# Two-layer decoder, last stage: masks and exponential sums of the attention scores move from TensorE to VectorE and ScalarE

## Chip, cores and metric

One Trainium2 chip, one of its cores. The metric is the device time of one launch in microseconds; less is better. A measurement is the median of several runs.

## The reference

Six residual sublayers over `x` (8 batches of 256 tokens, 512 wide, fp32), each followed by a layer norm: differential attention, a long convolution, a mixture of experts, causal attention with 16 heads, cross attention to a context, and a causal attention whose 16 heads share one key and value per token, chosen by a gate. The change is in the fourth and the sixth:

```python
scores = jnp.einsum('bhqd,bhkd->bhqk', q, k) * HD ** (-0.5)
scores = jnp.where(causal, jnp.float32(-1000000000.0), scores)
a = jax.nn.softmax(scores, axis=-1)
ctx = jnp.einsum('bhqk,bhkd->bhqd', a, v)
...
att = jnp.einsum('bhqd,bkd->bhqk', q, k_shared) * (1.0 / math.sqrt(hd))
att = jnp.where(causal[None, None, :, :], att, -jnp.inf)
att = jax.nn.softmax(att, axis=-1)
y = jnp.einsum('bhqk,bkd->bhqd', att, v_shared)
```

## The kernel before

The kernel runs five stages one after the other. The last one (`tail_stage`) does sublayers four to six from about 1180 us of the span to its end. It treats a batch of 256 tokens as a unit. P is the causal attention of the fourth sublayer, C the cross attention, H the gate and the shared keys and values of the sixth, A the attention over them. They are staggered: round r works on batch r of P, r - 1 of C, r - 2 of H and r - 3 of A. The loop `for r in range(2, B)` holds the rounds 2 to 7; rounds 0 and 1 and the end (A5, A6, A7 among it) are written out by hand.

Each engine has its own program, with the same rounds in an order written by hand, and waits on semaphores. TensorE writes to PSUM: four banks called `ring` that are claimed in turn for projections, transposes and weighted sums (a claim waits until the bank's last content was drained), and one group of four banks, `scores`, claimed by `quads`.

A unit of P or A has 16 heads in four blocks of four (`c`), each block with these steps:

- `score` (L1865 on): 16 small bf16 products by `add_masks` (L123) write the causal mask into `scores`, products of 256 (L1883) and 128 columns (L1886) add query times key. Queries lie on the partitions. The four heads of a block stand on four strips of 32 rows and run side by side; each fp32 product is two records in the trace.
- `maxima` (VectorE, L2603 and L2604): the negated row maxima into `negtop`, and the bank is released.
- After four blocks `split_top` (VectorE) writes the maxima as two bf16 parts, `shift` (TensorE, L1893) turns them, `take_shift` (ScalarE) copies them to `shiftT`.
- `scoreT` (L1905, L1909, L1912) computes the scores again with the keys on the partitions, with the shift added by a product with `pick16`. `exps` (ScalarE, L2394) takes their exponentials into `expT`. `causal` (GpSimd) zeroes the masked entries (L2310) and adds the two key halves of the later queries (L2315).
- `weigh` multiplies by the values (L1932), and by 32 columns of ones (L1935): these are the sums of the exponentials. `mix` (VectorE) takes their reciprocals (L2615) and multiplies (L2616) into `mixedT`.

Other steps named below: `cols` and `rows` are the projections (L191, L198), `turn` a transpose of a batch (L1848), `shared_out` the transposes of A's result, `cross_turn` those of C's probabilities, `turned` a wait for ScalarE's two copies of a turn. `norm` (L2583) applies a layer norm whose root comes from GpSimd (`root`, L2302); `gate_choice` (from L2631), `pick` and `gate_value` build the shared key and value on VectorE and drain H's banks. At the head of the stage GpSimd fetches rows, fills `pick16` by eight dependent selects (L2327), and only then does the first root.

## Time and profile before

| | |
|---|---|
| median of 3 runs | 2128.2 us (2126.52 to 2128.36) |
| span of the profiled execution | 2127.3 us |
| TensorE busy | 97% |
| VectorE busy | 53% |
| ScalarE busy | 24% |
| GpSimd busy | 27% |

The span is from the first to the last instruction of the profiled execution. TensorE's busy time is a union of records whose ends are modelled, so steps of TensorE are better measured from the start of one to the start of the next. A number in brackets behind an instruction is the engine's idle time before it, and what ended that.

### The profile page before, as it was taken

The page shows a single profiled execution, that of the slowest core. Times are in us where ns is not written, and L with a number is a line of the kernel's source. Part 1 is how long each engine was busy: PE and PEld are TensorE (multiplying, and loading weights), DVE is VectorE, ACT ScalarE, POOL GpSimd, SP SyncE. Part 2 cuts the span into 40 slices and gives each one's busy share as a digit, 9 for nine tenths or more (in the row PEclk, how much of TensorE's full clock was granted, in tenths as well). Part 3 has the DMA queues.
Part 4 walks back from the last instruction along what each step waited for, and adds up shares of the span by engine and source line. Part 5 has one row for each costly group of instructions (what it writes and reads, how often), then busy time and mean ns, then how long its engine had stood idle before and what let it go on. Part 6 is the DMA issues. An engine that isn't in the chain of part 4 may idle for free. (4 is left out here: it accounts for less than half of the span.)

```text
span 2127.3 us, 32323 instructions
## 1 busy us (share of the span) xinstructions
PE 2057.7 (97%) x13439; PEld 1194.6 (56%) x13439; DVE 1128.4 (53%) x1731; ACT 518.8 (24%) x791; POOL 580.5 (27%) x548
## 2 busy tenths in 40 slices
PE   7899999999999999999999999999999999999996
PEld 5444444334444557556566655766666666666664
DVE  2567777567777744122222334364646464736567
ACT  2445555440000121101011122122222222222211
POOL 2222222128999600111110312022222222121122
PEclk9999999999999999999999999999999999999998
DMA  5101111205111147321211602100010101000000
GB/s 161 48 1 55 55 56 45 87 38 210 40 43 44 35 156 277 126 65 65 65 65 55 222 3 99 50 31 21 17 44 1 60 1 41 1 31 12 1 11 21
DMA packets 66237, 130.81 MB, mean 61 GB/s; under 512 B 6480, under 2 KB 19920, under 8 KB 66096
## 3 DMA queue, kind: packets, MB, share of 16 engines
q1 hardware_dynamic: 45968, 77.49, 11.1%
q10 hardware_dynamic: 14448, 32.64, 4.3%
q0 software_dynamic: 5680, 18.62, 3.0%
q8 instruction: 111, 1.82, 0.4%
q14 instruction: 30, 0.25, 0.0%
HBM read 97.40 MB, written 41.81 MB: 65 GB/s over the span
## 5 line engine op out<-in xcount | busy, mean ns | idle before, releaser
L1033 PE MATMUL conv_conv<-kv,toep 128*128 128x512 f32 x576 | 247.6, 592 | 0.3 <-POOL kv L1067 0.3
L2615 DVE RECIPROCAL tail_inv<-tail_ring 128x256 f32<-128x256 f32 x63 | 110.7, 1757 | 188.8 <-PE tail_ring L1935 188.3
L1623 PE MATMUL moe_gu_ps<-gu,xT_tile 128*128 x608 | 192.4, 459 | 0.0
L1033 PEld LDWEIGHTS conv_conv<-kv,toep 128*128 128x128 f32 x576 | 109.4, 190 | 139.0 <-issue 129.6
L1067 POOL TENSOR_TENSOR kv<-vT,cT 128x512 f32<-128x512 f32 x128 | 147.0, 1172 | 15.8 <-PE conv_conv L1033 12.0
L2302 POOL TENSOR_TENSOR tail_rstd_x<-tail_rstd_x,const_minus_half 128x2 f32<-128x2 f32 x31 | 21.8, 702 | 469.6 <-DVE tail_rstd_x L2577 469.6
L1623 PEld LDWEIGHTS moe_gu_ps<-gu,xT_tile 128*128 128x128 f32 x608 | 112.3, 190 | 66.5 <-issue 17.8
L2310 POOL TENSOR_SCALAR_AFFINE_SELECT tail_expT<-tail_expT 128x1024 f32<-128x1024 f32 x64 | 71.5, 1119 | 242.1 <-ACT tail_expT L2394 242.0
L2603 DVE TENSOR_REDUCE tail_negtop<-tail_scores 128x4 f32<-128x1024 f32 x64 | 78.2, 1221 | 95.6 <-PE tail_scores L1886 95.4
L594 POOL TENSOR_SCALAR_AFFINE_SELECT front_expT<-front_expT 128x2048 f32<-128x2048 f32 x32 | 64.3, 2008 | 199.1 <-ACT front_expT L649 199.1
L1604 POOL DMA_INDIRECT xg<-x_after,tokens x37 | 35.0, 947 | 282.3 <-PE moe_xT_ps L1618 255.2
L1705 DVE TENSOR_TENSOR moe_hid<-moe_gu_ps,moe_silu 128x352 f32<-128x352 f32 x39 | 20.5, 525 | 170.7 <-PE moe_gu_ps L1623 170.7
L649 ACT ACTIVATE front_expT<-front_scores 128x2048 f32<-128x2048 f32 x48 | 90.1, 1878 | 78.3 <-PE front_scores L367 78.3
L1651 PE MATMUL moe_y_ps<-down,moe_hT 128*128 (+1 forms) x234 | 107.1, 593 | 0.7 <-ACT moe_hT L1691 0.7
L2394 ACT ACTIVATE tail_expT<-tail_scores 128x1536 f32<-128x1536 f32 x63 | 91.4, 1451 | 64.8 <-PE tail_scores L1912 64.8
L1674 ACT ACTIVATE moe_silu<-moe_gu_ps 128x352 f32<-128x352 f32 x39 | 18.1, 464 | 270.2 <-PE moe_gu_ps L1623 270.2
L770 DVE TENSOR_REDUCE front_negtop<-front_scores 128x8 f32<-128x2048 f32 x32 | 73.2, 2288 | 18.6 <-PE front_scores L335 18.4
L2315 POOL TENSOR_TENSOR tail_expT<-tail_expT 128x512 f32<-128x512 f32 x60 | 76.7, 1279 | 5.0
L1089 ACT COPY both<-conv_conv 128x512 f32<-128x512 f32 x32 | 18.7, 586 | 229.9 <-PE conv_conv L1033 211.0
L1717 DVE COPY moe_y<-moe_y_ps 128x512 f32<-128x512 f32 x39 | 27.0, 692 | 72.7 <-PE moe_y_ps L1651 72.7
L198 PE MATMUL tail_ring<-tail_gk,tail_xT 128*128 128x416 f32 (+1 forms) x256 | 63.4, 399 | 1.5 <-ACT tail_xT L2376 1.5
L1651 PEld LDWEIGHTS moe_y_ps<-down,moe_hT 128*128 128x128 f32 (+1 forms) x234 | 41.6, 191 | 38.5 <-issue 38.3
(394 smaller groups left out, 3912.2 us busy)
## 6 DMA issues: line engine op xcount, KB each, us to landing
toep<-toeplitz SPq DMA_DIRECT2D x32, 320.0 KB, 2.9
y_slots<-moe_y ACTq DMA_DIRECT2D x39, 256.0 KB, 2.0
gu<-in_L_ffn_gate_up_proj SPq DMA_DIRECT2D x5, 1408.0 KB, 12.5
toeplitz<-filt_rows SPq DMA_DIRECT2D x8, 768.0 KB
front_e<-in_ctx SPq DMA_DIRECT2D x8, 512.0 KB, 4.7
toeplitz<-filt_rows SPq DMA_DIRECT2D x16, 256.0 KB
x_after<-x SPq DMA_DIRECT2D x8, 512.0 KB, 5.0
tail_x<-x_after SPq DMA_DIRECT2D x8, 512.0 KB, 3.7
```

Source lines behind the costliest of these rows:

```text
L594: pool.affine_select(out=tile, in_=tile, compare_op=ALU.is_ge, fill=0.0, base=0, pattern=[[0, 16], [1, P]], channel_multiplier=-1).then_in ...
L649: act.activation(exp_buf(b, n)[:].rearrange("p g j q -> p g (j q)"), scores[:], ACT.Exp).then_inc(quads.drained_sem(key), 1)
L770: ins = dve.tensor_reduce(negtop[:, 1, n].rearrange("p (g a) -> p g a", a=2), scores[:].rearrange("p g (a k) -> p g a k", a=2), AX_X, ALU. ...
L1033: ins = pe.matmul(bank, toep[p][:, mat * P:(mat + 1) * P], kv[p][:, c].rearrange("p b j i -> p (b j i)"), start=n == 0, stop=n == len(PART ...
L1067: pool.tensor_tensor(kv[p][:, c], tokens_of(c, h), context_of(c, h, 3), ALU.mult).then_inc(kv_ready, 1)
L1623: ins = pe.matmul(gu_ps[:, s % 2, h, 0:HID], (xT if s else mid.xT_first)[:, c, :], wgu[c][:, e, h * HID:(h + 1) * HID], start=c == 0, stop ...
L1651: ins = pe.matmul(y_ps[:, s % 2, :], hT[0:w, n, :], wd[n][0:w, e, :], start=n == 0, stop=n == 2)
L2310: pool.affine_select(out=diagonal, in_=diagonal, compare_op=ALU.is_ge, fill=0.0, base=0, pattern=[[0, 8], [1, P]], channel_multiplier=-1). ...
L2315: pool.tensor_tensor(e[:, 3], e[:, 0], e[:, 2], ALU.add).then_inc(masked[kind], 1)
L2394: act.activation(exp_buf(kind, b, c)[:, 0:3].rearrange("p n g q -> p g n q"), quads.tile(key)[:, :, 0:3 * P].rearrange("p g (n q) -> p g n ...
L2603: dve.tensor_reduce(negtop[:, 1, heads_of(c)], scores[:, :, 0:S], AX_X, ALU.max, negate=True)
L2615: link.after(dve.reciprocal(inv[c % 2][:], bank[:, S:2 * S]))
```

## The change

It touches the P and A units of the full rounds, called `normal`: P2 to P7 and A0 to A4. There `score` writes no mask, and its products start the accumulation. `maxima` becomes eight operations a block (`PARTS`: two query tiles by four heads) that add the mask `wedge` to the scores, write the negated sum to SBUF (`hidden`) and accumulate the minimum into `negtop`. Behind each, ScalarE (`sums`) takes the exponential of that part in place and accumulates its sum into `esum`. After four blocks `take_logs` takes their logarithms, `split_top` subtracts them from the negated maxima and splits the result into three bf16 parts instead of two. The exponentials of the transposed scores are thereby probabilities: `weigh` has no product with ones, `mix` is a copy, and GpSimd adds no key halves. The other units (P0, P1, A5, A6, A7) keep their way, but also split in three. `hidden` shares space with the key sums of those. `wedge` and the picks are larger, and the picks take twelve selects.

The order changes with it: TensorE does a value projection ahead of each shift where it did it behind, and a turn or both `cross_turn` between the shift and the first transposed scores. ScalarE does the `sums` between its copies. VectorE does `split_top` behind the norm of x5 (A) and behind the residual rows of A, ahead of the gate choice (P). ScalarE preloads a table set.

```diff
-WEDGE = 96
+WEDGE = 128
...
-        split = st.sb("split", [P, NT, 4, 2, NG], BF16)
-        pick16 = st.sb("pick16", [P, 4, P], BF16)
+        split = st.sb("split", [P, NT, 4, 32], BF16)
+        picks = st.sb("picks", [P, 4, P], BF16)
...
-        expT = [st.sb(f"expT{p}", [P, 4, 4, P]) for p in range(3)]
+        expT = st.sb("expT", [P, 12, 4, P])
+        hidden = expT[:, 9:12].rearrange("p n g q -> p (n g q)").rearrange("p (g s) -> p g s", g=4)
+        esum, logs, total, rest = (st.sb(n, [P, NT, NG]) for n in ("esum", "logs", "total", "rest"))
...
+        normal = [unit for r in range(2, B) for unit in (("A", r - 3), ("P", r)) if unit[1] >= 0]
+        PARTS = [(t, g) for t in (1, 0) for g in range(4)]
...
-                    add_masks(pe, consts, lambda g, rows: bank[rows, g, P:3 * P].rearrange("p (a k) -> p a k", a=2), 2)
+                    bare = (kind, b) in normal
+                    if not bare:
+                        add_masks(pe, consts, lambda g, rows: bank[rows, g, P:3 * P].rearrange("p (a k) -> p a k", a=2), 2)
...
-                        pe.matmul(bank[:, g, 0:S], q[s, P:S], k[s, 0:S], start=False, stop=False, skip_group_check=True)
+                        pe.matmul(bank[:, g, 0:S], q[s, P:S], k[s, 0:S], start=bare, stop=bare, skip_group_check=True)
...
-                        ins = pe.matmul(bank[:, g, S:S + P], q[s, 0:P], k[s, 0:P], start=False, stop=True, skip_group_check=True)
+                        ins = pe.matmul(bank[:, g, S:S + P], q[s, 0:P], k[s, 0:P], start=bare, stop=True, skip_group_check=True)
                     ins.then_inc(quads.filled_sem((kind, "S", b, c)), 1)
...
-                        ins = pe.matmul(bank[:, n * P:(n + 1) * P], split[:, t].rearrange("p r a h -> p (r a h)"),
+                        ins = pe.matmul(bank[:, n * P:(n + 1) * P], split[:, t].rearrange("p r h -> p (r h)"),
...
-                    pe.wait_ge(masked[kind], 8 * b + c + 1 if last else 2 * (4 * b + c) + 2)
+                    bare = (kind, b) in normal
+                    pe.wait_ge(masked[kind], masks_ahead(kind, b, c) + (1 if last or bare else 2))
...
-                            pe.matmul(bank[32 * g:32 * g + 32, lo:S].rearrange("p (n q) -> p n q", q=P), v(kt, g), e[:, 0:1, g] if kt else e[:, 1:3, g],
-                                      start=kt == 0, stop=False, skip_group_check=True)
-                    for g in range(4):
-                        ins = pe.matmul(bank[32 * g:32 * g + 32, S:2 * S].rearrange("p (n q) -> p n q", q=P), ones32[:],
-                                        e[:, 1:3, g] if last else e[:, 1:4:2, g], start=False, stop=not last, skip_group_check=True)
+                            ins = pe.matmul(bank[32 * g:32 * g + 32, lo:S].rearrange("p (n q) -> p n q", q=P), v(kt, g),
+                                            e[:, 0:1, g] if kt else e[:, 1:3, g], start=kt == 0, stop=bare and kt == 1, skip_group_check=True)
+                    if not bare:
+                        for g in range(4):
+                            ins = pe.matmul(bank[32 * g:32 * g + 32, S:2 * S].rearrange("p (n q) -> p n q", q=P), ones32[:],
+                                            e[:, 1:3, g] if last else last_rows(kind, b, c)[:, :, g], start=False, stop=not last,
+                                            skip_group_check=True)
...
-                pe.wait_ge(pick_made, 9)
+                pe.wait_ge(pick_made, 13)
...
+                    if P_: rows("P", "v", p, 0, xT[p % 2], wide["wv"])
                     if A_: shift("A", a)
-                    if P_: rows("P", "v", p, 0, xT[p % 2], wide["wv"])
+                    if C_: turn("C", "x4", c)
                     if A_: scoreT("A", a, 0)
-                    if C_: turn("C", "x4", c)
...
@@ -2134,15 +2166,16 @@
                     if H_: turn("H", "x5", h)
                     if A_: shared_out(a)
                     if H_: turned("H", h); shared_keys(h, 0); gates(h)
+                    if H_: rows("H", "v", h, 0, xT[h % 2], wide["gv"])
                     if P_: shift("P", p)
-                    if H_: rows("H", "v", h, 0, xT[h % 2], wide["gv"])
+                    if C_:
+                        for t in range(NT):
+                            cross_turn(c, t)
                     if P_: scoreT("P", p, 0)
                     if H_: shared_keys(h, 1)
-                    if C_: cross_turn(c, 0)
                     if P_: scoreT("P", p, 1)
                     if H_: rows("H", "v", h, 1, xT[h % 2], wide["gv"])
                     if P_: weigh("P", p, 0)
-                    if C_: cross_turn(c, 1)
...
-                    if kind == "A" and b == B - 1:
+                    if (kind, b) == ("A", B - 1) or (kind, b) in normal:
                         return
-                    pool.wait_ge(masked[kind], 2 * (4 * b + c) + 1)
-                    pool.tensor_tensor(e[:, 3], e[:, 0], e[:, 2], ALU.add).then_inc(masked[kind], 1)
+                    pool.wait_ge(masked[kind], masks_ahead(kind, b, c) + 1)
+                    pool.tensor_tensor(key_sum(kind, b, c), e[:, 0], e[:, 2], ALU.add).then_inc(masked[kind], 1)
...
-                pool.memset(pick16[:], 0.0).then_inc(pick_made, 1)
-                for n in range(8):
-                    g, k = n // 2, n % 2
+                pool.memset(split[:], 0.0).then_inc(made, 1)
+                pool.memset(picks[:], 0.0).then_inc(pick_made, 1)
+                for n in range(12):
+                    g, k = n // 3, n % 3
                     pool.wait_ge(pick_made, n + 1)
-                    pool.affine_select(out=pick16[:], in_=pick16[:], compare_op=ALU.not_equal, fill=1.0, base=-(33 * g + 16 * k),
-                                       pattern=[[-4, 4], [0, P]], channel_multiplier=1).then_inc(pick_made, 1)
+                    pool.affine_select(out=picks[:], in_=picks[:], compare_op=ALU.not_equal, fill=1.0, base=-(32 * g + 4 * k),
+                                       pattern=[[-1, 4], [0, P]], channel_multiplier=1).then_inc(pick_made, 1)
...
+                def sums(kind, b, c):
+                    for i, (t, g) in enumerate(PARTS):
+                        key, h = (kind, "S", b, c), 4 * c + g
+                        if i < len(PARTS) - 1:
+                            act.wait_ge(topped, (len(PARTS) - 1) * place(kind, b, c) + i + 1)
+                        else:
+                            act.wait_ge(quads.drained_sem(key), quads.count(key))
+                        part = hidden[:, g, keys_of(t)]
+                        act.activation(part, part, ACT.Exp, bias=negtop[:, t, h:h + 1], scale=-1.0,
+                                       accum_out=esum[:, t, h:h + 1]).then_inc(summed, 1)
+
+                def take_logs(kind, b):
+                    act.wait_ge(summed, len(PARTS) * (place(kind, b, NC - 1) + 1))
+                    act.activation(logs[:], esum[:], ACT.Ln).then_inc(logs_ready, 1)
...
+                act.preload_act_table_set("natural_log_exp_and_others")
...
+                    if P_: take_turned("P", p)
+                    for j in range(2):
+                        if A_: sums("A", a, 2 * j)
+                        if P_: take(("P", "q", p, j), pair(qT["P"], j), SCALE)
+                        if A_: sums("A", a, 2 * j + 1)
+                        if P_ and j == 0: take(("P", "k", p, j), pair(kT["P"], j))
+                    if A_: take_logs("A", a)
                     if P_:
-                        take_turned("P", p)
-                        for j in range(2):
-                            take(("P", "q", p, j), pair(qT["P"], j), SCALE)
-                            take(("P", "k", p, j), pair(kT["P"], j))
+                        take(("P", "k", p, 1), pair(kT["P"], 1))
+                        take(("P", "v", p, 0), v_p[:, 0, :])
                     if A_: take_shift("A", a)
-                    if P_: take(("P", "v", p, 0), v_p[:, 0, :])
+                    if C_: take_turned("C", c)
                     if A_: exps("A", a, 0)
-                    if C_: take_turned("C", c)
                     if P_: take(("P", "v", p, 1), v_p[:, 1, :])
                     if A_: exps("A", a, 1)
                     if C_: take(("C", "v", c, 0), vx[:, 0, :])
                     if A_: exps("A", a, 2)
                     if C_: take(("C", "v", c, 1), vx[:, 1, :])
                     if A_: exps("A", a, 3)
-                    if C_:
-                        for j in range(2):
-                            take(("C", "q", c, j), pair(qx, j))
-                        for t in range(NT):
-                            cross_exp(c, t)
+                    if C_: take(("C", "q", c, 0), pair(qx, 0))
+                    sums("P", p, 0)
+                    if C_: take(("C", "q", c, 1), pair(qx, 1))
+                    sums("P", p, 1)
+                    if C_: cross_exp(c, 0)
+                    sums("P", p, 2)
+                    if C_: cross_exp(c, 1)
+                    if H_: take_turned("H", h)
+                    sums("P", p, 3)
+                    take_logs("P", p)
                     if H_:
-                        take_turned("H", h)
                         act.wait_ge(gate_exp_in, h + 1)
                         act.activation(gex[:], ranked[:], ACT.Exp).then_inc(gate_exp_out, 1)
-                    if P_:
-                        take_shift("P", p)
-                        exps("P", p, 0)
-                    if C_: take(("C", "p", c, 0), probT[:, 0].rearrange("p k q -> p (k q)"))
-                    if P_: exps("P", p, 1)
-                    if C_: take(("C", "p", c, 1), probT[:, 1].rearrange("p k q -> p (k q)"))
-                    if P_: exps("P", p, 2)
+                    take_shift("P", p)
+                    if C_:
+                        for t in range(NT):
+                            take(("C", "p", c, t), probT[:, t].rearrange("p k q -> p (k q)"))
+                    exps("P", p, 0)
+                    exps("P", p, 1)
+                    exps("P", p, 2)
                     if H_: take(("H", "q", h, 0), pair(qT["A"], 0), SCALE)
                     if P_: exps("P", p, 3)
...
+                    if (kind, b) in normal:
+                        at = place(kind, b, c)
+                        if at:
+                            dve.wait_ge(summed, len(PARTS) * at)
+                        for t, g in PARTS:
+                            h = 4 * c + g
+                            ins = dve.tensor_tensor_reduce(out=hidden[:, g, keys_of(t)], in0=scores[:, g, keys_of(t)],
+                                                           in1=consts["wedge"][:, 0 if t else P:2 * P], scale=-1.0, scalar=-NEVER,
+                                                           op0=ALU.add, op1=ALU.min, accum_out=negtop[:, t, h:h + 1])
+                            if (t, g) != PARTS[-1]:
+                                ins.then_inc(topped, 1)
+                        ins.then_inc(quads.drained_sem(key), 1)
+                        return
                     dve.tensor_reduce(negtop[:, 1, heads_of(c)], scores[:, :, 0:S], AX_X, ALU.max, negate=True)
                     ins = dve.tensor_reduce(negtop[:, 0, heads_of(c)], scores[:, :, S:S + P], AX_X, ALU.max, negate=True)
                     ins.then_inc(quads.drained_sem(key), 1)
                     dve.wait_ge(quads.drained_sem(key), quads.count(key))
...
                 def split_top(kind, b):
-                    top = negtop[:].unsqueeze(2).to_broadcast([P, NT, 4, NG])
-                    link.after(dve.tensor_copy(split[:, :, :, 0, :], top))
-                    dve.tensor_tensor(split[:, :, :, 1, :], top, split[:, :, :, 0, :], ALU.subtract).then_inc(split_ready[kind], 1)
+                    whole = negtop
+                    if (kind, b) in normal:
+                        whole = total
+                        dve.wait_ge(logs_ready, normal.index((kind, b)) + 1)
+                        link.after(dve.tensor_tensor(total[:], negtop[:], logs[:], ALU.subtract))
+
+                    def by_strip(m):
+                        return m[:].rearrange("p t (c r) -> p t r c", r=4)
+
+                    def part(n):
+                        return split[:, :, :, 4 * n:4 * n + 4]
+
+                    link.after(dve.tensor_copy(part(0), by_strip(whole)))
+                    link.after(dve.tensor_tensor(by_strip(rest), by_strip(whole), part(0), ALU.subtract))
+                    link.after(dve.tensor_copy(part(1), by_strip(rest)))
+                    dve.tensor_tensor(part(2), by_strip(rest), part(1), ALU.subtract).then_inc(split_ready[kind], 1)
 
                 def mix(kind, b, c):
                     bank = filled((kind, "W", b, c))
+                    if (kind, b) in normal:
+                        dve.tensor_copy(mixedT[:, c, :], bank[:, 0:S]).then_inc(ring.drained_sem((kind, "W", b, c)), 1)
+                        return
...
-                dve.wait_ge(made, 2)
+                dve.wait_ge(made, 3)
...
                     if A_:
                         for n in range(1, 4):
                             maxima("A", a, n)
-                        split_top("A", a)
                     if H_: norm("x5", h)
+                    if A_: split_top("A", a)
...
-                    if P_:
-                        maxima("P", p, 3)
-                        split_top("P", p)
+                    if P_: maxima("P", p, 3)
                     if A_:
                         for t in range(NT):
                             ins = add_rows("A", "o", "x6", "x5", a, t)
                             ins.then_inc(ring.drained_sem(("A", "o", a, t)), 1)
                         dve.wait_ge(ring.drained_sem(("A", "o", a, 1)), ring.count(("A", "o", a, 1)))
+                    if P_: split_top("P", p)
```

## Rows read from the trace of the kernel before

**Rows 1.** Busy time by stretch: stretch, length, busy PE, PEld, DVE, ACT, POOL, clock, DMA.
```profile
1400.00:1500.00 100.00, 100.00 (x839) 65.49 (x838) 51.41 (x85) 21.37 (x33) 20.17 (x19) 1.00 0.08 27
...
1800.00:1900.00 100.00, 100.00 (x846) 66.18 (x845) 57.13 (x91) 20.99 (x33) 16.58 (x15) 1.00 0.05 17
```

**Rows 2.** Waits of TensorE from 1400 us on: total, times, longest.
```profile
PE tail_ring L1893 <- DVE tail_split L2611: 2.6, 1, 2.6
```

**Rows 3.** Groups by line and shape, 1250 to 2127 us: busy us, mean ns.
```profile
L2615 DVE RECIPROCAL tail_inv<-tail_ring 128x256 f32<-128x256 f32 x62 | 108.9, 1757 | 173.6 <-PE tail_ring L1935 173.1 <-PE tail_ring L1939 0.3
...
L1935 PE MATMUL tail_ring<-tail_expT,tail_ones 128*32 128x256 f32 x504 | 38.8, 379 | 0.0
...
L2376 ACT COPY tail_qx<-tail_ring 128x512 f32<-128x512 f32 x16 | 9.4, 587 | 58.4 <-PE tail_ring L191 58.4
```

**Rows 4.** Timeline of TensorE, first scores of an A unit: start, duration, line.
```profile
1648.40 0.33 PE L123 MATMUL tail_scores<-const_wedge,const_ident_bf 32*32 32x256 bf16 x16
1648.66 0.71 PE L1883 MATMUL tail_scores<-tail_kT_a,tail_qT_a 32*128 32x256 f32 x8
...
1649.52 3.72 PE L191 MATMUL tail_ring<-tail_xT,early_wq 128*128 128x256 f32 x16
1653.17 0.33 PE L123 MATMUL tail_scores<-const_wedge,const_ident_bf 32*32 32x256 bf16 x16
```

**Rows 5.** Timeline of TensorE, two weighings of P0 and what follows.
```profile
1256.96 0.61 PE L1935 MATMUL tail_ring<-tail_expT,tail_ones 128*32 128x256 f32 x8
1257.39 0.83 PE L1932 MATMUL tail_ring<-tail_expT,tail_v_p 128*32 128x256 f32 x16
1258.04 0.61 PE L1935 MATMUL tail_ring<-tail_expT,tail_ones 128*32 128x256 f32 x8
1258.59 3.70 PE L2015 MATMUL tail_ring<-raw_wo,cT 128*128 128x512 f32 x8
```

**Rows 6.** Timeline of TensorE, from a P unit's last scores to its shift.
```profile
1599.39 1.09 PE L1848 MATMUL tail_ring<-const_ident,tail_x 128*128 128x128 f32 x8
1600.32 1.04 PE L2001 MATMUL tail_ring<-const_ident,tail_mixedT 128*128 128x128 f32 x8
...
1605.90 0.33 PE L1893 MATMUL tail_ring<-const_ident_bf,tail_split 128*128 128x128 bf16 x3
```

**Rows 7.** Timeline of VectorE in a full round: mix, maxima, gate, norm.
```profile
1583.44 0.42 DVE L2616 TENSOR_TENSOR tail_mixedT<-tail_ring,tail_inv 128x256 f32<-128x256 f32 x1
1583.78 1.21 DVE L2603 TENSOR_REDUCE tail_negtop<-tail_scores 128x4 f32<-128x1024 f32 x1
...
1606.17 0.39 DVE L2631 COPY tail_allowed<-tail_ring 128x224 f32<-128x224 f32 x1 [3.03 <-PE tail_ring L198]
...
1610.39 0.75 DVE L2657 SCALAR_TENSOR_TENSOR tail_allowed<-tail_ring,tail_gval,tail_ind 128x512 f32<-128x512 f32 x1
...
1650.04 1.22 DVE L2603 TENSOR_REDUCE tail_negtop<-tail_scores 128x4 f32<-128x1024 f32 x1
...
1651.89 1.00 DVE L2583 TENSOR_SCALAR tail_x<-tail_x,tail_moments_x,tail_rstd_x 128x512 f32<-128x512 f32 x2
```

**Rows 8.** Timeline of ScalarE, an accumulating exponential and the next one.
```profile
1299.06 0.69 ACT L2400 ACTIVATE tail_probs<-tail_ring,tail_xneg 128x512 f32<-128x512 f32 x1 [4.39 <-DVE tail_xneg L2620]
1299.64 0.19 ACT L2400 ACTIVATION_READ_ACCUMULATOR tail_probs<-tail_ring,tail_xneg 128x1 f32 x1
1299.74 1.44 ACT L2394 ACTIVATE tail_expT<-tail_scores 128x1536 f32<-128x1536 f32 x1
```

**Rows 9.** Timeline at the head of the stage: GpSimd's selects and root, TensorE's turn.
```profile
1186.62 7.15 POOL L2327 TENSOR_SCALAR_AFFINE_SELECT tail_pick<-tail_pick 128x512 bf16<-128x512 bf16 x8
...
1194.39 0.72 POOL L2302 TENSOR_TENSOR tail_rstd_x<-tail_rstd_x,const_minus_half 128x2 f32<-128x2 f32 x1 [0.62 <-DVE tail_rstd_x L2577]
...
1197.24 1.04 PE L1848 MATMUL tail_ring<-const_ident,tail_x 128*128 128x128 f32 x8
```

**Rows 10.** Timeline of ScalarE, the stage's one table load.
```profile
1236.29 1.28 ACT L2394 ACT_TABLE_LOAD   x1
```

20 lines of the change are left out of this document (18 added, 2 removed).

## Prediction

> **What bounds the kernel now.** I read the busy time by stretches first. From 1400 to 1900 us TensorE is busy for 100.00 of every 100 us at a granted clock of 1.00, VectorE for 51 to 58, ScalarE for 21 to 24, GpSimd for 17 to 26 (the first and the last of five stretches stand) [rows 1]. A busy TensorE need not be an efficient one, so I read next who waited for whom: the waits of TensorE for another engine lie before 1331 us and after 2049 us; the largest is 2.6 us for the last split [rows 2]. In the full rounds nothing holds TensorE back. So a stretch of matrix work taken out there is worth its own length, as long as no new wait replaces it. What VectorE and GpSimd lose is worth nothing by itself.
>
> **What is removed from TensorE.** The change touches 11 units (P2 to P7, A0 to A4) of four blocks: 44 blocks. Counts agree with the code: 8 records of the ones product a block, 504 of them in the window for its 63 blocks of that form [rows 3]; the masks are 16 a block. I take start-to-start times, since the modelled ends overlap. The masks start at 1648.40 and the products after them at 1648.66: 0.26 us [rows 4]. The ones product takes 0.43 us where another weighing follows (1256.96 to 1257.39) and 0.55 us where a product of another shape follows (1258.04 to 1258.59) [rows 5]. Of the 0.55, I count 0.12 as the price of changing shape, which the value product will then pay in its place, so I take 0.43. Sum: 0.69 x 44 = 30.4 us. The upper end is 0.81 x 44 = 35.6. The lower is 0.59 x 44 = 26.0: the first fp32 weights of a block may no longer load under the masks, some 0.1 us each.
>
> **What VectorE does instead.** Before, a block costs it two reductions, 1.85 us from start to next (1650.04 to 1651.89) [rows 7]. After, it is eight fused operations, four of 256 and four of 128 columns. The trace has no fused one. The nearest is the product 128x256 from PSUM: 0.42 us long, the next operation starts 0.34 after it (1583.44, 1583.78); the slope to the 1024-wide reduction, (1.21 - 0.42)/768, is 1.03 ns a column, so 0.21 for 128 columns [rows 7]. That is 2.2 us a block with an accumulator for nothing. ScalarE's accumulating ACTIVATE shows a second instruction that adds 0.10 us (1299.64 to 1299.74) [rows 8]; with that on each part, 3.0 us. The upper bound is a reduction of its own behind each part, 8 x 0.24 more: 4.1 us. I take 3.0, since a fused operation passes over its data once. The reciprocals (1.76 us each [rows 3]) go, so VectorE as a whole gets freer by over 1 us a block. What counts is the release of the score bank: the next scores need it 3.65 us after the last ones (1649.52 to 1653.17) [rows 4], and 3.0 fits. It doesn't quite at the head of an A unit: VectorE comes 0.5 us late to the first block (1650.04 against 1649.52), and has the two norms (1.00 us when undisturbed) to do ahead of the second [rows 4, 7]. I charge 0.4 us to each of five A units: 2.0 us.
> The Trainium skill ("VectorE: DVE Perf Modes", section "Two Vector instructions with no wait between them") also says that an operation that writes its accumulator out is two instructions. No row of VectorE here shows it; the 3.0 rests on ScalarE's row alone.
>
> **What ScalarE does instead.** It gets eight exponentials with a sum per block. The one accumulating ACTIVATE, 512 wide, takes 0.68 us to the next start (1299.06 to 1299.74), of which its own stream is 512 x 0.83 ns, by the slope between the 512-wide copy (0.587) and the 1536-wide exponential (1.44) [rows 3, 8]. So 256 columns cost 0.47 us, 128 cost 0.36: 3.3 us a block. Without overlap between main part and read (0.19) it is 4.9 us. I take 3.3: the row shows the overlap. From scores complete to the last sum: 0.45 for VectorE's first part, then 3.3, so 3.8 us. TensorE's scores come every 3.65 + 0.86 = 4.5 us in an A unit, and 5.2, 5.2 and 4.5 us in a P unit; one copy of 0.5 us lies between two blocks and runs while VectorE makes the next first part. So ScalarE keeps pace, and the wait of each block for the sums of the one before (they share a buffer) is over in time.
>
> **The longer chain to the shift.** Let T be the end of a unit's fourth scores. A unit: last sum T+3.8, logs 4.1, the norms of x5 on VectorE beside it, then five small VectorE operations of some 0.2 us (the 224-wide copy of 0.39 [rows 7] less its slope): split ready by T+5.2 to 6. TensorE reaches the shift after a key product and, now, a value product, T+7.2: hidden, with over 1 us to spare. Behind the shift stands the turn (0.93 us [rows 6]), just long enough for ScalarE's copy. P unit: ScalarE must first take two turned banks (T+2.1), sums to 5.4, logs 5.8, split 6.9. TensorE comes to the shift at 6.5 (1599.39 to 1605.90) plus the value product of 3.6, T+10.1: hidden. But the gate choice now queues behind the split on VectorE. Before it began at T+6.8 (1606.17) and freed the bank of the value product 5.0 later (1610.39 + 0.75) [rows 6, 7]; now T+11.9. TensorE needs that bank for the second half of the keys after shift, two turns and one transposed block, T+12.3. Hidden, but with only 0.4 us left: this is the tightest place. I charge nothing.
>
> **The rest.** GpSimd loses 44 sums of keys: covered, TensorE waited for none in the full rounds. At the head of the stage it makes twelve selects where it made eight; 7.15/8 = 0.89 us each, so 3.6 us more ahead of the root (1194.39) that the first norm needs. Of that, 0.6 us was idle there and about 0.8 lies between the end of that norm and the turn (1197.24) [rows 9], so 2.2 us of new idle time. The split in three parts puts two more small operations into the chain of the last unit, where TensorE already waits [rows 2]: 0.4 us. The table load moves to where ScalarE is idle: nothing.
>
> **Sum.** -30.4 + 2.0 + 2.2 + 0.4 = -25.8 us. The profiled execution spans 2127.3 us, 0.9 under the median of 2128.2; I subtract from the median: 2102.4 us.
>
> **Rivals.** (1) VectorE's fused part is dearer. At 4.1 us a block each of 23 gaps of 3.65 us between scores overruns by 0.5: +11.5, so 2114 us. For it: nothing shows this operation; against: one pass over the data. The skill's section "The DRAIN you can't avoid" of the same page would have the next operation wait until the one before has left the pipeline; the rows show it 0.08 us earlier (0.42 long, next start after 0.34), and by the page the block is some 0.6 us dearer.
> (2) ScalarE doesn't overlap main part and read: 4.9 us a block. Then blocks come every 5.4 us against 4.5, the last sum of an A unit is some 4.3 us later against 1.9 of room: 2.4 x 5; a P unit loses about as much in the chain that ends in the gate choice, x 6. Together +26: 2128.6 us, no change.
> (3) The slower side, same place: if each of the eight parts also pays for its own semaphore hand-over, 5.3 us a block. Each further 1 us costs 5 x 4 + 6 x 3 = 38 us, so +15 on (2): 2144 us. It decides from 4.9 us (break-even) and is measurable from 5.0. For it: eight waits a block and no work between them; against: the start of 1299.74 right behind a read.
> (4) The logarithm doesn't share a table with the exponential: two loads a unit, 1.28 us each [rows 10]. In an A unit the slack takes it; in a P unit 0.9 of it shows, x 6: 2108 us. The skill ("ScalarE: Activation LUTs", section "Table sets: the hidden batching unit") names a set that holds both, which speaks against it; no run here shows a logarithm.
>
> **How the numbers follow.** Forecast as summed: 0.62. Rival 1: 0.15. Rival 2: 0.07. Rival 3: 0.10. Rival 4: 0.06. Low end: 35.6 saved, 2.6 added: 2095. High end of the forecast and rivals 1 and 4 with the small saving (4.4 less): 2118. Range 2094 to 2119; rivals 2 and 3 stay outside. A measurement here can tell about 0.2%, 4.3 us, from no change. Faster 0.83, same 0.07, slower 0.10.
>
> **What would show it.** Right: in full rounds the scores' first product directly behind a projection, no ones product, TensorE still at 100 of 100 us, and each round with eight blocks 5 to 6 us shorter. VectorE's block from first to last part: 3.0 us; over 3.6 is rival 1, seen as TensorE's scores waiting for VectorE. ScalarE's block: 3.3 us; near 5 is rival 2 or 3, seen as the shift, or the second half of the keys, waiting for VectorE. Table loads inside rounds are rival 4. An idle 2 us before the first turn is the select chain.

## The result, and the profile after

| | before | after |
|---|---|---|
| median | 2128.3 us | 2097.4 us (2097.1 to 2100.8, 4 runs) |
| profiled execution, span | 2127.3 us | 2098.9 us |
| last stage in that execution, from its first fetch of `picked_y` | 946.3 us (from 1181.1) | 918.3 us (from 1180.6) |
| busy PE / DVE / ACT / POOL | 2058 / 1128 / 519 / 581 us | 2026 / 1072 / 676 / 525 us |

The ratio of the times is 0.9861, 95% interval 0.9847 to 0.9875: 1.4% faster, by some 30 us, against 25.8 forecast. In the profiled executions of this document the last stage starts anywhere between 1176.8 and 1183.3 us of the span, so from here on I compare the last stage alone where microseconds count: 27.9 us shorter. Within the stage the traces are finer than the medians: the first four of the rounds that hold eight blocks take 111.16 us each before, and 105.53 each after.

The page of after, busy time by engine (us, share of the span, instructions):

```profile
PE 2026.2 (97%) x12383; PEld 1179.3 (56%) x12383; DVE 1071.6 (51%) x2346; ACT 676.1 (32%) x1506; POOL 524.8 (25%) x509
```

Busy time by stretch after (stretch, its length, busy PE, PEld, DVE, ACT, POOL, clock, DMA share, GB/s), the first and the last as in [rows 1], and one full round:

```profile
1400.00:1500.00 100.00, 99.99 (x691) 66.08 (x690) 47.52 (x204) 52.86 (x166) 14.26 (x15) 1.00 0.08 27
...
1800.00:1900.00 100.00, 99.99 (x692) 64.59 (x691) 44.86 (x184) 49.88 (x148) 10.75 (x11) 1.00 0.05 17
...
1650.00:1755.00 105.00, 104.99 (x736) 68.64 (x728) 52.77 (x212) 53.97 (x164) 15.32 (x16) 1.00 0.10 31
```

TensorE is still busy all the time at full clock, with fewer instructions. ScalarE's share has more than doubled (21 to 53 in a hundred), and TensorE doesn't wait for it there: from 1440 to 1860 us its trace has no wait for another engine. TensorE's timeline after, an A unit's head, one weighing, and the same head a round later:

```profile
1424.79 0.71 PE L1912 MATMUL tail_scores<-tail_kT_a,tail_qT_a 32*128 32x256 f32 x8
...
1425.65 3.72 PE L191 MATMUL tail_ring<-tail_xT,early_wq 128*128 128x256 f32 x16
1429.30 0.71 PE L1912 MATMUL tail_scores<-tail_kT_a,tail_qT_a 32*128 32x256 f32 x8
...
1461.08 0.86 PE L1962 MATMUL tail_ring<-tail_expT,tail_v_a 128*32 128x256 f32 x16
1461.87 0.34 PE L1934 MATMUL tail_scores<-tail_shiftT,tail_picks 32*128 32x384 bf16 x4
...
1530.32 0.71 PE L1912 MATMUL tail_scores<-tail_kT_a,tail_qT_a 32*128 32x256 f32 x8
```

Scores to next scores took 4.77 us with the masks (1648.40 to 1653.17 [rows 4]) and take 4.51 now (1424.79 to 1429.30): 0.26 us. A weighing up to the next instruction takes 0.79 us (1461.08 to 1461.87). A round of eight blocks took 111.16 us (from the line below to 1648.40 [rows 4]) and takes 105.53 (1424.79 to 1530.32): 5.63 us less, where 8 x 0.69 = 5.5 were forecast. Five such rounds and round 2, with its four blocks (2.5 us), make 30.7 us, where 30.4 were forecast. Against that the turn ahead of round 2 comes 1.7 us later behind the stage's first fetch (167.6 us against 165.9), and the end, from A5's shift on, is 1.0 longer (124.2 against 123.2). The three make 27.9, the whole of what was measured. TensorE's timeline before, the head of the A unit ahead of that of [rows 4]:

```profile
1537.24 0.33 PE L123 MATMUL tail_scores<-const_wedge,const_ident_bf 32*32 32x256 bf16 x16
```

VectorE's timeline at that A unit's first two blocks (main part and read of the accumulator alternate, equal rows left out):

```profile
1426.47 0.42 DVE L2667 CUSTOM_DVE_ANT_0 tail_expT<-tail_scores,const_wedge 128x256 f32<-128x256 f32 x1
1426.82 0.08 DVE L2667 DVE_READ_ACCUMULATOR2_ANT tail_negtop<- 128x1 f32 x1
1426.82 0.42 DVE L2667 CUSTOM_DVE_ANT_0 tail_expT<-tail_scores,const_wedge 128x256 f32<-128x256 f32 x1
...
1428.49 0.29 DVE L2667 CUSTOM_DVE_ANT_0 tail_expT<-tail_scores,const_wedge 128x128 f32<-128x128 f32 x1
...
1428.70 1.00 DVE L2641 TENSOR_SCALAR tail_x<-tail_x,tail_moments_x,tail_rstd_x 128x512 f32<-128x512 f32 x2
1430.69 0.42 DVE L2667 CUSTOM_DVE_ANT_0 tail_expT<-tail_scores,const_wedge 128x256 f32<-128x256 f32 x1 [1.00 <-ACT tail_expT L2439]
```

The block takes 2.23 us (1426.47 to 1428.70), the lower bound of the prediction: the read is 0.08 us long and lies wholly beside the next main part, both start at 1426.82. The second block waits 1.00 us for ScalarE's sums of the first, and still ends at 1432.92, ahead of TensorE's next scores at 1433.82.

ScalarE's timeline, the sums of that block and what follows:

```profile
1426.94 0.51 ACT L2439 ACTIVATE tail_expT<-tail_expT,tail_negtop 128x256 f32<-128x256 f32 x1 [1.41 <-DVE tail_negtop L2667]
1427.35 0.19 ACT L2439 ACTIVATION_READ_ACCUMULATOR tail_expT<-tail_expT,tail_negtop 128x1 f32 x1
1427.44 0.49 ACT L2439 ACTIVATE tail_expT<-tail_expT,tail_negtop 128x256 f32<-128x256 f32 x1
...
1430.46 0.58 ACT L2412 ACTIVATE tail_qT_p<-tail_ring 128x512 f32<-128x512 f32 x1
1431.16 0.51 ACT L2439 ACTIVATE tail_expT<-tail_expT,tail_negtop 128x256 f32<-128x256 f32 x1
```

3.52 us a block (1426.94 to 1430.46), 0.49 for each part of 256 columns; each read adds 0.09 (1427.35 to 1427.44). With the copy, block follows block after 4.2 us (1426.94 to 1431.16): less than TensorE's 4.51, so ScalarE keeps pace.

### The profile page after: what moved, and what is told of

Read it like the earlier page. It is cut to its first block, busy times and chain, and to the rows that moved or that the text cites. A ratio compares the mean times of both kernels' runs of the same rounds, so it can differ in the third digit from the quotient of the medians.

```text
span 2098.9 us, 31516 instructions
## 1 busy us (share of the span) xinstructions
PE 2026.2 (97%) x12383; PEld 1179.3 (56%) x12383; DVE 1071.6 (51%) x2346; ACT 676.1 (32%) x1506; POOL 524.8 (25%) x509
## 4 chain that ended last, share of the span: by engine, by line
PE 55%; DVE 2%; POOL 1%; issue 1%; ACT 1%; DMA 0%; POOLq 0%; DVEq 0%
PE tail_ring L198 14%; PE tail_ring L191 11%; PE moe_gu_ps L1623 9%; PE moe_y_ps L1651 5%; PE tail_ring L2005 3%; PE tail_ring L1962 2%; PE tail_scores L1912 2%; PE tail_ring L1982 1%; PE tail_ring L1985 1%; PE tail_scores L1938 1%; PE tail_ring L1875 1%; PE moe_xT_ps L1618 1%; PE tail_scores L1934 1%; PE tail_scores L1915 1%; PE tail_scores L1941 1%
## 5 line engine op out<-in xcount | busy, mean ns | idle before, releaser
L2439 ACT ACTIVATE tail_expT<-tail_expT,tail_negtop 128x128 f32<-128x128 f32 (+1 forms) x352 | 155.0, 443 | 28.4 <-DVE tail_negtop L2667 27.0
L2667 DVE CUSTOM_DVE_ANT_0 tail_expT<-tail_scores,const_wedge 128x128 f32<-128x128 f32 (+1 forms) x352 | 101.3, 353 | 58.3 <-PE tail_scores L1915 51.4
L2700 DVE COPY tail_mixedT<-tail_ring 128x256 f32<-128x256 f32 x44 | 18.7, 424 | 152.2 <-PE tail_ring L1962 151.3
L2439 ACT ACTIVATION_READ_ACCUMULATOR tail_expT<-tail_expT,tail_negtop 128x1 f32 x352 | 66.3, 188 | 0.0
```

The lines of the kernel that those rows point to most:

```text
L2439: act.activation(part, part, ACT.Exp, bias=negtop[:, t, h:h + 1], scale=-1.0, accum_out=esum[:, t, h:h + 1]).then_inc(summed, 1)
L2667: ins = dve.tensor_tensor_reduce(out=hidden[:, g, keys_of(t)], in0=scores[:, g, keys_of(t)], in1=consts["wedge"][:, 0 if t else P:2 * P], ...
```

## The experiments

Each is an edit of the changed kernel that leaves its outputs as they are: a mask that comes back is added a second time, and the result of everything else that comes back or is added isn't used. "Stage" is the last stage in the one profiled execution, against 918.3 after. "Round" is a round with eight blocks, from the first scores of an A unit to those of the next, the first of them in each trace: 111.16 before, 105.53 after.

| run | edit | median us | ratio to before [95%] | stage | round |
|---|---|---|---|---|---|
| e1 | masks back | 2109.7 | 0.991 [0.9893, 0.9926] | +11.1 | 107.59 |
| e2 | ones product back | 2119.2 | 0.9956 [0.9939, 0.9972] | +19.0 | 108.98 |
| e10 | both back | 2129.8 | 1.0005 [0.9994, 1.0015] | +30.0 | 111.05 |
| e3 | reciprocals back on VectorE | 2109.8 | 0.9914 [0.9898, 0.9931] | +8.3 | 107.21 |
| e11 | e3, copy ahead of the sums | 2110.7 | 0.9918 [0.9897, 0.9939] | +11.0 | 107.27 |
| e12 | copy ahead of the sums alone | 2106.4 | 0.9897 [0.9876, 0.9918] | +8.6 | 106.55 |
| e4 | shift ahead of the value product | 2120.8 | 0.9964 [0.995, 0.9978] | +17.3 | 108.26 |
| e5 | selects after the first root | 2099.7 | 0.9868 [0.9844, 0.9892] | -1.8 | 105.53 |
| e6 | VectorE +3 operations a block | 2103.4 | 0.9879 [0.9856, 0.9902] | +2.5 | 106.05 |
| e7 | VectorE +7 | 2156.1 | 1.0131 [1.0112, 1.015] | +55.8 | 115.57 |
| e8 | ScalarE +2 | 2107.2 | 0.9911 [0.9889, 0.9932] | +9.0 | 107.12 |
| e9 | ScalarE +5 | 2147.1 | 1.0083 [1.0066, 1.01] | +48.5 | 113.66 |

The kernel before took 2127.2 to 2129.2 us beside them.

### Is the gain the matrix time, and is it additive? (e1, e2, e10)

```diff
 # e1
-                    if not bare:
-                        add_masks(pe, consts, lambda g, rows: ...)
+                    add_masks(pe, consts, lambda g, rows: ...)
+                    bare = False
 # e2, behind the value products
+                    if bare:
+                        for g in range(4):
+                            ins = pe.matmul(bank[32 * g:32 * g + 32, S:2 * S]..., ones32[:],
+                                            e[:, 1:3, g], start=False, stop=True, skip_group_check=True)
 # e10: both
```

> The changed kernel with TensorE's sixteen mask products a block put back in the full rounds (the mask is then added twice, which changes nothing in the result). Theory, the gain is TensorE's own matrix time: 44 blocks x 0.26 us = +11.4 us on the changed kernel, 2097.4 to 2109. Rival, the gain comes from the reciprocals that VectorE no longer does and the masks were cheap beside them: no more than +3 us. Rival, the first weights now load late and the masks were worth less (0.16 each): +7 us.

> The changed kernel with the product with the ones put back in the full rounds, its result unused. Theory: 44 x 0.43 = +18.9 us, to 2116; 44 x 0.55 = +24.2 if the price of changing shape belongs to it. Rival, the gain is VectorE's: under +5 us.

> The changed kernel with both the masks and the product with the ones back on TensorE, everything else as changed. Theory: 44 x 0.69 = +30.4 us, 2128, so no difference from the kernel before that can be measured; the new order and VectorE's relief are worth nothing by themselves. Rival, they are worth something of their own: 2120 or less.

Measured in the stage: +11.1, +19.0, +30.0. Busy time of the same full round, e1 first, then e2:

```profile
1650.00:1755.00 105.00, 104.99 (x848) 68.01 (x850) 50.71 (x200) 52.23 (x158) 15.35 (x16) 1.00 0.08 24
```

```profile
1650.00:1755.00 105.00, 104.99 (x769) 67.47 (x769) 48.90 (x198) 52.26 (x160) 14.63 (x15) 1.00 0.08 25
```

No new idle time in either: the whole price is matrix time, 11.4 and 18.9 us by the prediction's 0.26 and 0.43 x 44. That rules out the rivals of e1 and e2 (VectorE's relief as the gain, and masks worth only 0.16 us). The two add up, and with both back the kernel is at the time of before, although VectorE then still has its shorter work and GpSimd none of the sums of keys. Its round takes 111.05 us (the two lines below, TensorE's timeline of e10) against 111.16, so no more than 0.1 us a round is gained on balance from elsewhere; its stage is 2.1 us longer than that of before, by what the change costs at the head and at the end.

```profile
1423.46 0.33 PE L123 MATMUL tail_scores<-const_wedge,const_ident_bf 32*32 32x256 bf16 x16
...
1534.51 0.33 PE L123 MATMUL tail_scores<-const_wedge,const_ident_bf 32*32 32x256 bf16 x16
```

### Is VectorE's relief worth nothing? (e3, e11, e12)

```diff
 # e3, in the mix of a normal unit
                     if (kind, b) in normal:
+                        link.after(dve.reciprocal(inv[c % 2][:], bank[:, 0:S]))
                         dve.tensor_copy(mixedT...
```

> The changed kernel with a reciprocal of 256 columns (1.76 us) put back in front of each of the 44 copies of mix; its result is unused. Theory, VectorE's relief is worth nothing by itself: within 3 us of the changed kernel. Rival, it carried the gain: +15 us or more.

It cost 8.3 us in the stage, 12 in the medians: each of the five rounds is 1.68 us longer. My theory falls. TensorE in a full round of e3, then its waits in the whole stage (total us, times, longest):

```profile
1650.00:1755.00 105.00, 103.74 (x719) 67.20 (x717) 65.46 (x214) 52.15 (x159) 15.31 (x16) 1.00 0.10 31
```

```profile
PE tail_ring L1982 <- ACT tail_qx L2410: 5.2, 7, 0.8
PE tail_ring L198 <- ACT tail_xT L2410: 4.8, 9, 0.8
```

After has 1.1 us in 2 times and 3.1 in 4 on these two. TensorE is idle 1.26 us in each full round, though VectorE is busy only 65 of 105. The chain, read from the timelines of VectorE, ScalarE and TensorE of e3:

```profile
1579.34 1.76 DVE L2700 RECIPROCAL tail_inv<-tail_ring 128x256 f32<-128x256 f32 x1 [0.87 <-PE tail_ring L1962]
```

```profile
1576.63 0.51 ACT L2439 ACTIVATE tail_expT<-tail_expT,tail_negtop 128x256 f32<-128x256 f32 x1 [2.82 <-DVE tail_negtop L2667]
...
1580.15 0.56 ACT L2410 COPY tail_qx<-tail_ring 128x512 f32<-128x512 f32 x1
```

```profile
1580.97 1.97 PE L1982 MATMUL tail_ring<-tail_ctxq,tail_xT 128*128 128x256 f32 x8 [0.83 <-ACT tail_qx L2410]
```

TensorE's first scores of that P unit, in e3 and then in the changed kernel, where the first sums start at 1574.23:

```profile
1573.90 0.71 PE L1912 MATMUL tail_scores<-tail_kT_p,tail_qT_p 32*128 32x256 f32 x8
```

```profile
1572.76 0.71 PE L1912 MATMUL tail_scores<-tail_kT_p,tail_qT_p 32*128 32x256 f32 x8
```

In e3 a reciprocal stands on VectorE ahead of the P block's fused part (the one ahead of this first block began at 1574.04). So ScalarE's sums of block 0 start at 1576.63, 2.82 us after ScalarE was free; behind TensorE's scores of that block they come 2.7 us (1573.90), in the changed kernel 1.5 (1572.76 to 1574.23). The copy of C's second query half, which stands behind them in ScalarE's queue, comes at 1580.15. TensorE waits 0.83 us for it. Is it this place in the queue that costs, or is the delay only seen there first? Two kernels put the copy ahead of the sums:

```diff
                     if C_: take(("C", "q", c, 0), pair(qx, 0))
+                    if C_: take(("C", "q", c, 1), pair(qx, 1))
                     sums("P", p, 0)
-                    if C_: take(("C", "q", c, 1), pair(qx, 1))
```

> The kernel with the reciprocals back on VectorE, and ScalarE's copy of the cross unit's second query half moved ahead of the sums of the P unit's first block. Theory: the reciprocals cost 8.3 us of the last stage because ScalarE's queue is in order and this copy stands behind sums that wait for VectorE; TensorE's seven waits for the cross query (5.2 us against 1.1) then go, and the stage comes out 3 to 5 us shorter than with the reciprocals alone (922 to 924 us against 926.6), about 2105 to 2107 in all. Rival: the copy is only where the delay shows first, ScalarE is late anyhow because its sums start late, and the same microseconds come back as waits for tail_xT, the split or the mask: 926 to 928 us of stage, 2109 to 2111.

> The changed kernel with the same move of the copy alone, no reciprocals. Both theories: the copy waits for its product (1577.3 in the profile), so the P unit's first sums start some 3.5 us later than now; ScalarE's block of 3.5 us stands against a period of 5.3 us there and catches up by the fourth block, so nothing changes: stage 918 to 920 us, 2096 to 2100 in all. If the sums don't catch up, the P unit's split comes after TensorE's shift and each full round costs up to 1 us: up to 2104.

The rival holds in e11: its round takes 107.27 us, as e3's 107.21, so the move gives nothing back; of the 2.7 us that its stage is longer than e3's, 2.4 lie ahead of round 3. e12 is a miss of both: the move alone costs 8.6 us, 1.0 in each of the five rounds and 3.6 ahead of round 3, where its trace also has a mean granted clock of 0.98 (1335 to 1440 us; after: 1.00), worth 1.7 us by e4's rounds below. TensorE's largest wait in the stage in e12, and how it arises, on ScalarE, VectorE and TensorE:

```profile
PE tail_scores L1912 <- DVE tail_negtop L2667: 5.4, 6, 2.2
```

```profile
1581.95 0.58 ACT L2410 COPY tail_qx<-tail_ring 128x512 f32<-128x512 f32 x1 [4.72 <-PE tail_ring L191]
1582.43 0.51 ACT L2439 ACTIVATE tail_expT<-tail_expT,tail_negtop 128x256 f32<-128x256 f32 x1
```

```profile
1586.19 0.42 DVE L2667 CUSTOM_DVE_ANT_0 tail_expT<-tail_scores,const_wedge 128x256 f32<-128x256 f32 x1 [2.99 <-ACT tail_expT L2439]
```

```profile
1577.33 0.71 PE L1912 MATMUL tail_scores<-tail_kT_p,tail_qT_p 32*128 32x256 f32 x8
...
1588.64 0.71 PE L1912 MATMUL tail_scores<-tail_kT_p,tail_qT_p 32*128 32x256 f32 x8 [0.64 <-DVE tail_negtop L2667]
```

The copy waits 4.72 us for TensorE, and the sums start 5.1 us behind TensorE's scores (1577.33 to 1582.43) where they started 1.5 behind them: 3.6 us later, as both theories had reckoned. What they left out is the buffer that the blocks share. ScalarE makes the delay good only over the next blocks, and VectorE's second block must wait 2.99 us for these sums, so it frees the score bank late, and TensorE waits 0.64 us for the bank. So the P phase holds three queues that hand work to each other in order, and a delay on VectorE (e3, 1.3 us at the first sums) or on ScalarE (e12, 3.6 us) comes out on TensorE: in e3 at the cross scores, in e11 at the score bank (6.7 us in 11 waits). The waits for the cross query and for `tail_xT` that e3 adds to after's come to 5.8 of its 8.3 us (4.1 and 1.7); the rest lies in the same five rounds and isn't placed.

### Which room lies before the shift, and at the head? (e4, e5)

```diff
 # e4
-                    if P_: rows("P", "v", p, 0, xT[p % 2], wide["wv"])
                     if A_: shift("A", a)
+                    if P_: rows("P", "v", p, 0, xT[p % 2], wide["wv"])
 ...
-                    if H_: rows("H", "v", h, 0, xT[h % 2], wide["gv"])
                     if P_: shift("P", p)
+                    if H_: rows("H", "v", h, 0, xT[h % 2], wide["gv"])
 # e5: memset(picks) and its twelve selects moved behind root("x3", 0) and fetch(1)
```

> The changed kernel with each shift back ahead of the value projection, so 3.6 us less cover for the chain of sums, logs and split. In the trace of the changed kernel the split of an A unit is ready 5.6 us after the last scores end, and TensorE would come for it at 3.6; that of a P unit at 6.8 against 6.5. Theory: 5 x 2.1 + 6 x 0.3 = +12 us, seen as waits of the shift for the split, 2.1 us each. Rival, the chain is hidden without the new order too: within 2 us.

> The changed kernel with the twelve selects of GpSimd behind the first root and the second fetch. Theory: the 1.5 us that TensorE is idle before the first turn go, 2097.4 to 2096, and nothing else waits for the picks before 1230 us. Rival, the second fetch or the first masking by GpSimd becomes late: no gain or a loss of about 1 us.

e4, the shift of an A unit; its waits for the split; two full rounds:

```profile
1447.91 0.34 PE L1922 MATMUL tail_ring<-const_ident_bf,tail_split 128*128 128x128 bf16 x3 [1.98 <-DVE tail_split L2695]
```

```profile
PE tail_ring L1922 <- DVE tail_split L2695: 13.4, 9, 2.9
```

```profile
1545.00:1650.00 105.00, 102.69 (x722) 66.47 (x722) 50.91 (x196) 51.31 (x156) 15.39 (x16) 1.00 0.08 23
1650.00:1755.00 105.00, 102.69 (x704) 65.85 (x702) 49.13 (x190) 50.90 (x151) 14.70 (x15) 0.98 0.06 19
```

The split waits went from 3.3 to 13.4 us: 1.98 in an A unit, 0.15 in a P unit. So the value product that the change put there hides 2 us an A unit, and the chain to the split is as long as the prediction had it. The stage lost more than the waits, and more than the 12 us expected: TensorE was idle 2.3 us a round, and three of the five rounds are 2.7 us longer than those of after (108.26 against 105.53). The other two are 1.7 us longer still (109.94 against 108.26): in them the mean granted clock was 0.98, so for a small part of them 1.2 GHz was granted instead of 2.4. 5 x 2.7 + 2 x 1.7 = 16.9 of 17.3.

e5 takes the idle time ahead of the first turn away: the turn comes 16.2 us after the first fetch, as in the kernel before, against 17.9 after. 1.8 us in the stage fits, and its rounds are those of after, but between the medians (2099.7 and 2097.4, other chips) nothing is to be seen of it.

### How much room have VectorE and ScalarE? (e6 to e9)

```diff
 # e6: with "if t == 0:", 3 more a block; e7: without, 7 more
                             if (t, g) != PARTS[-1]:
                                 ins.then_inc(topped, 1)
+                                if t == 0:
+                                    link.after(dve.tensor_tensor(inv[0]..., scores[:, g, keys_of(t)],
+                                                                 consts["wedge"]..., ALU.add))
 # e8: n = 2, e9: n = 5, in the sums
+                        if 2 <= i < 2 + n:
+                            if extras:
+                                act.wait_ge(extra, len(extras))
+                            act.copy(inv[0][:], consts["wedge"][:, 0:S]).then_inc(extra, 1)
+                            extras.append(i)
```

> The changed kernel with three more additions of 128 columns a block on VectorE between its fused parts, results unused: its block goes from 2.2 to about 3.2 us, a little over the 3.0 that the prediction took. The prediction's step charged 0.4 us at the head of each A unit for 3.0: +2 to +3 us. Rival, at 3.2 the bank is still free in time because the head of the unit has more room than reckoned: within 1 us.

> The changed kernel with seven more additions a block on VectorE (four of 256, three of 128 columns, each waiting for its own end): a block of about 5.0 us. Rival 1's rule, a gap of 3.65 us between scores overruns: 23 x 1.4 + 10 x 0.7 = +39 us, to 2136, seen as TensorE's score products waiting for VectorE. Rival, the overrun is caught up later in a round: under +20.

> The changed kernel with two more copies of 256 columns a block on ScalarE between its sums: a block of about 4.1 to 4.2 us in place of 3.5. By the changed kernel's trace the chain of an A unit has 1.35 us of room at the shift and grows by 2.3, that of a P unit has 0.3 us of room at the second half of the keys and grows by 1.0: 5 x 1.0 + 6 x 0.7 = +9 us, to 2107. The prediction's slope (38 us for each us a block, from about 0.3 us above its 3.3): +11. Rival, ScalarE has room to spare: within 2 us.

> The changed kernel with five more copies of 256 columns a block on ScalarE: a block of about 5.1 us, near rivals 2 and 3. By their rule the whole gain is gone and the kernel is slower than before: chain of an A unit 4.8 us late x 5, of a P unit 2.9 x 6, +41 us, to 2138. Rival, the scores don't wait and only the shifts do: about +25, no change against the kernel before.

TensorE's waits for the score bank in e6 and in e7, then the head of an A unit in e6, on TensorE and on VectorE:

```profile
PE tail_scores L1912 <- DVE tail_negtop L2667: 2.2, 5, 0.4
```

```profile
PE tail_scores L1912 <- DVE tail_negtop L2667: 44.9, 32, 2.4
```

```profile
1426.64 3.72 PE L191 MATMUL tail_ring<-tail_xT,early_wq 128*128 128x256 f32 x16
1430.80 0.71 PE L1912 MATMUL tail_scores<-tail_kT_a,tail_qT_a 32*128 32x256 f32 x8 [0.44 <-DVE tail_negtop L2667]
```

```profile
1427.46 0.42 DVE L2667 CUSTOM_DVE_ANT_0 tail_expT<-tail_scores,const_wedge 128x256 f32<-128x256 f32 x1
```

With a VectorE block of some 3.2 us, five waits of 0.4 us come, one at the head of each A unit: close to the prediction's 2.0 us, which the real block of 2.23 doesn't pay. The place is not quite the one that the prediction gave: the wait stands before the second scores, because VectorE began the first block 0.8 us after TensorE had done with it (1427.46 against 1426.64), and the two norms ahead of the second block held nothing up. The round is 0.5 us longer; the medians don't tell e6 from after. With 5.0 us (0.805 and 0.53 a part, the last without its extra) TensorE waits in 32 gaps, 1.4 us each, and the kernel is 1.3% slower than before. That is rival 1's place; my price for this dose (2136) was low, as it counted 23 gaps in full and 10 in half, and left out the other waits and a clock of 0.98 to 0.99 in two rounds.

ScalarE's extra copies cost 0.3 us each. With 4.1 us a block the stage lost 9.0 us, as expected; e8's waits for the split, then e9's four largest waits (5.0 us a block):

```profile
PE tail_ring L1923 <- DVE tail_split L2701: 6.4, 7, 2.9
```

```profile
PE tail_ring L1923 <- DVE tail_split L2701: 15.7, 7, 2.9
PE tail_scores L1913 <- DVE tail_negtop L2673: 9.4, 10, 1.1
PE tail_ring L1983 <- ACT tail_qx L2411: 8.3, 7, 1.9
PE tail_ring L198 <- ACT tail_xT L2411: 6.4, 9, 2.4
```

Between the two doses the slope is (48.5 - 9.0)/0.9 = 44 us for each us of block, where rival 3 had 38. But e9's trace holds three stretches of 105 us with a mean granted clock of 0.98 (1335 to 1440, 1545 to 1650, 1755 to 1860 us) and e8's none; at 1.7 us each they are 5 of the 48.5, and without them the slope is some 38. The loss starts lower than rival 3 said: on a straight line between the doses before's time is reached at about 4.5 to 4.6 us a block, not 4.9 (9.0 us at 4.1, and the other 27.9 - 9.0 = 18.9 at 44 or 38 us for each further us). No dose lies between the two.

## Why the prediction was right

The forecast of 2102.4 us stood 5 us above the 2097.4 measured. 2.1 of the 5 are placed in the last stage (27.9 for 25.8). The other 2.9 are not: the profiled executions differ by 28.4 us where the medians differ by 30.9, and after's profiled execution was the longest of its four (2100.8).

- **What is removed:** right, in place and size. 0.26 and 0.43 us a block, 5.63 a round for 5.5; e1, e2 and e10 give each term its value by itself.
- **VectorE's block and the 2.0 us at the A units:** a term mis-sized. I put ScalarE's 0.10 us for a read on VectorE's eight parts, and took 3.0 us; it was 2.23, the lower bound worked out from [rows 7] alone. The 0.4 us x 5 that followed from 3.0 was not paid; e6 shows the rule near its size (5 waits, 2.2 us at 3.2), but by the first block's late start and not by the norms. Rival 1's other ground, that an operation waits until the one before has left the pipeline, isn't seen either: the parts are 0.42 us long and start 0.345 us apart. The 2.0 us that weren't paid are the largest part of the miss in the stage. The sentence that VectorE gets freer by over 1 us a block didn't follow from 3.0 (1.85 + 1.76 - 3.0 = 0.6) and came true by the shorter block: 1.4 us.
- **ScalarE's block:** 3.52 us for 3.3; the overlap of main part and read from [rows 8] held (0.09 each). Rivals 2 and 3 needed a block without it.
- **The chain to the shift:** A unit, split ready at T+5.6 (1439.20 to 1444.84) for T+5.2 to 6, with 1.35 us to spare before the shift at 1446.19. P unit, split at T+6.8 for 6.9. The tightest place, the bank of the shared values, had 0.3 us left for 0.4: the operation at 1494.16 ends at 1494.91, TensorE's product starts at 1495.24 without a wait.

```profile
1494.16 0.75 DVE L2744 SCALAR_TENSOR_TENSOR tail_allowed<-tail_ring,tail_gval,tail_ind 128x512 f32<-128x512 f32 x1
```

- **The head:** 2.2 us forecast; the turn waited 1.5 and comes 1.7 later after the fetch, and all of the 1.7 is left at round 2. The twelve selects took 10.23 us, 3.1 more than the eight [rows 9] where I had reckoned 3.6, which is the 0.5 us too much; the root followed at once:

```profile
1186.36 10.23 POOL L2361 TENSOR_SCALAR_AFFINE_SELECT tail_picks<-tail_picks 128x512 bf16<-128x512 bf16 x12
1196.56 0.72 POOL L2335 TENSOR_TENSOR tail_rstd_x<-tail_rstd_x,const_minus_half 128x2 f32<-128x2 f32 x1
```

- **The end:** 0.4 us forecast, 1.0 measured. The last split's wait grew from 2.6 [rows 2] to 2.94 us, and A6's shift waits 0.33 where it didn't wait; the other 0.4 us lie behind TensorE's last product (8.3 before, 8.7 after) and aren't placed.
- **Table loads (rival 4):** the stage has one, at 1179.41, just ahead of its first fetch, and the logarithms none. The table holds both functions, as the Trainium skill ("ScalarE: Activation LUTs", section "Table sets: the hidden batching unit") says; the trace agrees.
- **"What VectorE and GpSimd lose is worth nothing by itself":** wrong for VectorE. The kernel before carried the reciprocals behind TensorE's back; the changed one wouldn't (e3: 8.3 us), since its sums on ScalarE hang on VectorE, and the delay reaches TensorE through the copies behind them or, with one of these moved, through the score bank (e11). So the relief is no gain of its own (e10), but a condition for keeping the gain. The prediction's sum had the reciprocals gone, and so came out right without having seen this; that much of it is luck. No run puts the reciprocals at another place in VectorE's order, so whether they could be hidden stays open.
- **The rivals' threshold:** e8 and e9 put the break-even of ScalarE's block near 4.5 to 4.6 us, not 4.9, so the real 3.52 stood some 1 us below it. It had no room for free: at 4.1 us 9.0 of the 27.9 us were gone.

## What to carry to other kernels

Where one engine is busy all the time, work taken off it is worth its start-to-start time, and putting each removed part back by itself shows it. What decides is whether the engines that take over keep pace block by block: compare their block with the period of the bound engine (here 3.5 us plus a copy against 4.5), not their share of the span. In queues that hand work to each other in order, look also at what stands behind each new wait and at who waits for the buffer: four reciprocals of 1.76 us in each unit, on an engine that was busy 65 of 105 us, made each round 1.7 us longer, and one copy placed earlier made it 1.0 us longer.

## What the runs showed of the hardware

- VectorE's fused operation with an accumulator written out is two records, as the Trainium skill ("VectorE: DVE Perf Modes", section "Two Vector instructions with no wait between them") says; the second (0.08 us) added nothing from start to start (0.345 us for 256 columns from PSUM, 0.21 for 128).
- On ScalarE the same read is 0.19 us long and adds 0.09. An accumulating exponential in SBUF took 0.49 us for 256 columns and 0.385 for 128, a copy of 256 columns 0.3.
- VectorE's norm took 656 ns in the mean of 58 after, 806 before, without any edit of its own, in a stage in which GpSimd has less to do. It isn't TensorE's products: in e10, with the masks and the ones back, the mean is 651 (of 62). No run takes GpSimd's share and the new order apart.
- With TensorE idle 2.3 us in each 105 us (e4), the mean granted clock was 0.98 in two of five rounds, and each of these took 1.7 us longer than the others; with 1.3 us (e3) it was 1.00 in all. With 3 us idle from 1335 to 1440 us it was 0.98 in e12 and 1.00 in e11, so the idle time alone doesn't say whether the clock falls.
